# Inverting denominators inside the attentions, four load buffers in the first mixing stage, clipping at the scaled maximum

## The chip, the cores and the metric

The kernel runs on one core of one Trainium2 chip. The measure is the time of one execution on the device in microseconds. A core has TensorE (PE), VectorE (DVE), ScalarE (ACT), GpSimd (POOL), SyncE (SP), which issues most DMAs, and 16 DMA engines.

## The reference

The input x is 8 x 1024 tokens of 256 numbers, float32. Four blocks follow one another, each as `x = x + layernorm(block(layernorm(x)))`:

```python
# 1 attention over a latent of 64, 16 heads of 16, causal softmax
attn = softmax(where(causal, Q @ K.T / 4, -inf)); out = (attn @ V) @ W_o
# 2 feed-forward with ternary weights and a low-rank addition
h = bitlinear(x, w_fc) + gate * (x @ v.T @ fast_b.T @ u.T); out = bitlinear(max(h, 0)**2, w_proj)
# 3 linear attention, second-order features of q and k, causal sums
y = num / (phi_q . cumsum(phi_k) + 1e-5); out = y @ Wo.T
# 4 ternary weights, input scaled by the largest absolute value of the whole tensor
gamma = max(abs(xn)); xq = clip(xn * 128 / gamma, -128 + 1e-5, 128 - 1e-5)
out = (xq @ w_q) * (gamma * beta / 128)
```

Both attentions need a division: the numerator of each head and token by a denominator of that head and token. Block 4 needs one number, gamma, from the whole tensor before its first product.

## The kernel before

`build` (L63) runs passes one after another; between two passes all engines meet, and semaphores of a pass are cleaned up. x stays in SBUF (64 tiles of 128 tokens). The passes are: weights, latent projections, attention with softmax (`attend_pass`, tiles a_*), first mixing stage (`mix_pass`, tiles m_*), feed-forward, features, attention without softmax (tiles b_*), second mixing stage, ternary stage.

**The attentions.** A unit is four heads of one batch, 32 units in all; units run in rounds of three, the last two stand outside of the loop (`all_units`). A unit has 10 steps. TensorE computes the scores of a step two steps ahead of the one that it weighs with the values. In the softmax attention ScalarE takes the exponential and VectorE takes maxima for later units. In the second, ScalarE squares three of four heads and VectorE the fourth (L976, L979); GpSimd masks the steps on the diagonal (L919). Each half of a unit ends with a copy of its sums from PSUM (L938), which SyncE stores in DRAM (L867). These sums hold, for each head, 16 rows of numerators and one of denominators. At its end SyncE waits until the last store has landed.

**The mixing stages.** Work goes in 16 groups of 512 tokens, two for a batch. SyncE loads the denominators of all batches (L1159, 64 KB each), VectorE adds 1e-5 in the second stage (L1210) and inverts (L1212), SyncE stores the inverses in DRAM (L1163) and loads them again, repeated for the 16 rows of each head (L1175). Numerators come through L1170. A group needs two DMAs of numerators and two of inverses, 256 KB each, into one of two buffers. GpSimd multiplies (L1271), TensorE projects (L1324) into one of two sets of banks, VectorE takes statistics from PSUM (L156, L160), ScalarE the root (L166), VectorE the reciprocal (L171), a product of mean and divisor (L1229), the addition to x (L1231) and the shift (L1236). GpSimd's multiplication waits for the loads, for the projection two groups before and for the shift three groups before. The helper `streamed` writes the order: VectorE's step n is add(n-1), then measure(n). The second mixing stage also normalises x for block 4, writes it turned into `flipped` (L1302) and takes the maximum of each group (L1253).

**The ternary stage.** VectorE reduces the 16 maxima to one a partition (L1809), GpSimd reduces over the partitions (L1854), VectorE derives a factor and gains (L1811 to L1815). Per group ScalarE multiplies `flipped` by the factor (L1864), VectorE clips (L1824), TensorE projects (L1891), VectorE takes statistics, root on ScalarE, scales on VectorE (L171, L1836 to L1840), ScalarE copies with scale and offset (L1875), VectorE adds to x (L1847), and SyncE stores the output (L1796). VectorE's step n is clip(n), measure(n-1), add(n-3), scales(n-1). Two sets of PSUM banks alternate: a projection waits for the copy of two groups before.

## Time and profile before

| | us |
|---|---|
| median of 3 runs (2794.3 to 2799.74) | 2794.38 |
| profiled execution, its time / its span | 2794.65 / 2792.9 |
| PE busy in the span | 2454.0 (88%) |
| DVE busy | 2199.0 (79%) |
| ACT busy | 1767.6 (63%) |
| POOL busy | 562.1 (20%) |
| last attention copy to first feed-forward statistics (first mixing stage) | 1154.24 to 1257.74 |
| last copy of the second attention to the ternary stage's first instruction | 2543.59 to 2694.40 |
| ternary stage to the end | 2694.40 to 2792.9 |

Rows of the order of instructions give start, duration (both us), engine, line, operation, output, inputs, shapes and count; in brackets stand the idle time of the engine before it and what ended it. SPq and ACTq are instructions that issue a DMA; their duration is that of the issue.

### The profile page before, as it was taken

Reading aid. Unit: us, or ns where it says so; the run is one execution under the profiler, and the core shown is the slowest. Engines: PE = TensorE matmul, PEld = TensorE weight load, DVE = VectorE, ACT = ScalarE, POOL = GpSimd, SP = SyncE. Lnnn points to the kernel's source line nnn. Section 1 sums busy time; section 2 is a strip of 40 time slices with the busy share of each in tenths; the row PEclk is TensorE's granted clock in tenths of the full one; section 3 lists DMA queues with packets and bytes.
Section 4 is the critical chain, followed back from the end, with each engine's and each line's share of the span. In section 5 each row is a group of like instructions: output and inputs, shape, how many; then the busy total and the mean of one; then the engine's idle time right before and its main releaser. Section 6 shows DMA issues by size and latency. Waiting matters only on the chain. (4 is left out here: it accounts for less than half of the span.)

```text
span 2792.9 us, 57214 instructions
## 1 busy us (share of the span) xinstructions
PE 2454.0 (88%) x15239; PEld 1155.9 (41%) x15239; DVE 2199.0 (79%) x5740; ACT 1767.6 (63%) x2700; POOL 562.1 (20%) x644
## 2 busy tenths in 40 slices
PE   5888999999999999578999997994999999996756
PEld 2442333333333333254666664663333333333645
DVE  6887999899999898286777767996666676666968
ACT  2452666666666666316777755884778788873546
POOL 1543111111111111240000000223222222222300
PEclk8996999999999999898999998997999999998879
DMA  6985353535454543360000002556866776664503
GB/s 187 287 280 122 77 108 81 105 84 103 86 102 87 102 87 83 85 182 1 0 0 0 0 0 68 188 188 184 162 144 142 148 145 144 141 138 118 149 8 117
DMA packets 224106, 309.46 MB, mean 111 GB/s; under 512 B 32416, under 2 KB 170352, under 8 KB 211952
## 3 DMA queue, kind: packets, MB, share of 16 engines
q1 hardware_dynamic: 223616, 307.47, 45.6%
q10 hardware_dynamic: 432, 1.31, 0.2%
q8 instruction: 25, 0.41, 0.1%
q14 instruction: 33, 0.27, 0.0%
HBM read 181.29 MB, written 126.88 MB: 110 GB/s over the span
## 5 line engine op out<-in xcount | busy, mean ns | idle before, releaser
L947 ACT ACTIVATE a_p<-psum 128x1024 f32<-128x1024 f32 (+1 forms) x640 | 567.3, 942 | 303.9 <-PE psum L1045 303.7
L947 ACT ACTIVATE b_p<-psum 128x512 f32<-128x512 f32 (+2 forms) x640 | 444.2, 750 | 145.1 <-PE psum L1045 142.0
L999 DVE CUSTOM_DVE_ANT_0 a_dump<-psum,a_bias 128x128 bf16<-128x128 f32 (+3 forms) x1024 | 446.3, 488 | 56.5 <-PE psum L1034 48.1
L997 DVE TENSOR_REDUCE a_peak<-psum 128x1 f32<-128x512 f32 x512 | 334.7, 688 | 27.6 <-PE psum L1034 25.0
L976 DVE COPY b_twin<-psum 128x512 f32<-128x512 f32 (+1 forms) x320 | 204.0, 637 | 164.5 <-PE psum L1045 161.2
L1045 PE MATMUL psum<-b_qs,b_ks 96*128 96x512 bf16 (+3 forms) x1536 | 307.1, 330 | 28.6 <-DMA b_vs<-values 28.6
L1061 PE MATMUL psum<-b_p,b_vs 128*32 128x512 f32 (+3 forms) x3072 | 314.7, 497 | 6.3 <-POOL b_p L919 6.2
L919 POOL TENSOR_SCALAR_AFFINE_SELECT a_p<-a_p 128x512 f32<-128x512 f32 x256 | 162.3, 634 | 753.7 <-ACT a_p L947 742.0
L1034 PE MATMUL psum<-a_ks,a_qs 96*128 96x128 bf16 (+2 forms) x1008 | 277.4, 333 | 19.3 <-DVE a_peak L999 13.9
L919 POOL TENSOR_SCALAR_AFFINE_SELECT b_p<-b_p 128x512 f32<-128x512 f32 x256 | 159.3, 634 | 441.1 <-DVE b_p L979 429.8
L1045 PE MATMUL psum<-a_qs,a_ks 98*128 98x512 bf16 x1008 | 234.2, 328 | 13.0 <-DMA a_qs<-a_rows 10.8
L1045 PEld LDWEIGHTS psum<-b_qs,b_ks 96*128 96x128 bf16 x1536 | 115.3, 98 | 291.0 <-issue 168.8
L979 DVE SCALAR_TENSOR_TENSOR b_p<-psum,b_twin 128x512 f32<-128x512 f32 (+1 forms) x320 | 204.4, 639 | 33.3
L1522 PE MATMUL psum<-f_xt,w_fc 128*128 128x512 f32 x512 | 225.3, 598 | 3.0 <-ACT f_hid L1463 2.8
L1061 PE MATMUL psum<-a_p,a_vs 128*32 128x512 f32 x2016 | 205.8, 496 | 0.5 <-POOL a_p L919 0.3
L1666 POOL TENSOR_TENSOR g_parts<-g_rest,g_parts 128x2048 bf16<-128x2048 f32 x16 | 66.0, 4127 | 629.7 <-DVE g_parts L1654 629.7
L1324 PE MATMUL psum<-wo,m_att 128*128 128x256 f32 x512 | 127.4, 406 | 58.5 <-POOL m_att L1271 40.0
L1034 PEld LDWEIGHTS psum<-a_ks,a_qs 96*128 96x128 bf16 x1008 | 83.9, 97 | 219.6 <-DVE a_peak L999 121.6
L1533 PE MATMUL psum<-w_proj,f_parts 128*128 128x256 bf16 x1536 | 170.3, 273 | 1.4 <-DVE f_scaled L1411 1.4
L1034 PE MATMUL psum<-first_k,first_q 96*128 96x128 bf16 (+3 forms) x528 | 151.4, 345 | 18.6 <-SPq L878 8.3
L1533 PEld LDWEIGHTS psum<-w_proj,f_parts 128*128 128x128 bf16 x1536 | 150.2, 98 | 19.4 <-DVE f_scaled L1411 1.7
L1400 DVE TENSOR_TENSOR f_rest<-f_sq,f_parts 128x512 f32<-128x512 f32 x128 | 88.5, 691 | 77.0 <-ACT f_sq L1471 76.0
(197 smaller groups left out, 3647.3 us busy)
## 6 DMA issues: line engine op xcount, KB each, us to landing
qk_parts<-l_parts SPq DMA_DIRECT2D x96, 256.0 KB, 3.2
qk_parts<-g_parts SPq DMA_DIRECT2D x96, 256.0 KB, 2.6
values<-l_vx SPq DMA_DIRECT2D x64, 256.0 KB, 3.4
sums<-a_osb SPq DMA_DIRECT2D x64, 256.0 KB, 2.1
m_num<-sums SPq DMA_DIRECT2D x64, 256.0 KB, 3.8
m_inv<-reciprocals SPq DMA_DIRECT2D x64, 256.0 KB, 4.6
values<-g_vx SPq DMA_DIRECT2D x64, 256.0 KB, 3.0
sums<-b_osb SPq DMA_DIRECT2D x64, 256.0 KB, 2.1
```

The costliest lines, as they stand in the source:

```text
L919: pool.affine_select(out=diag, in_=diag, compare_op=ALU.is_ge, fill=0.0, base=0, pattern=[[0, HPU], [1, P]], channel_multiplier=-1).then_i ...
L947: act.activation(p[s % SLOTS][:, 2 * k:2 * k + heads, cols], m.psum[:, at:at + heads, cols], ACT.Exp if softmax else ACT.Square, scale=z.D ...
L976: dve.tensor_copy(twin[s % 2][:, cols], bank).then_inc(twin_ready, 1)
L979: dve.scalar_tensor_tensor(out=p[s % SLOTS][:, 3, cols], in0=bank, scalar=1.0 / z.DK, in1=twin[s % 2][:, cols], op0=ALU.mult, op1=ALU.mult ...
L997: last = dve.tensor_reduce(dst, piece, AX.X, ALU.max)
L999: last = dve.tensor_tensor_reduce(dump[c % SRING][:, at:at + w], piece, bias[:, 512 - w:], 1.0, NEG, ALU.add, ALU.max, dst)
L1034: last = pe.matmul(m.bank[SB + c % SRING][:, at:at + w], qs[r][0:STACK, hd, qt * P:(qt + 1) * P], ks[r][0:STACK, hd, h * 512:h * 512 + w], ...
L1045: last = pe.matmul(m.bank[score_bank(r, s, hd)][:, at:at + w], ks[r][OPERAND, hd, kt * P:(kt + 1) * P], qs[r][OPERAND, hd, h * 512 + q:h * ...
L1061: last = pe.matmul(m.bank[OB[h]][32 * hd:32 * hd + 32, q:q + w], vs[r][:, kt, 32 * hd:32 * hd + 32], p[s % SLOTS][:, hd, at:at + w], start ...
L1324: last = pe.matmul(bank, att[u][:, c, t * P:(t + 1) * P], wo[:, c, :], start=(c == 0), stop=(c == DC - 1))
L1522: last = pe.matmul(m.bank[F0 + j % 4], m.w_fc[:, c, j * P:(j + 1) * P], xt[u][:, c, :], start=(c == 0), stop=(c == DC - 1))
L1533: last = pe.matmul(bank, parts[u][:, part, j, t * P:(t + 1) * P], m.w_proj[:, j, :], start=(part == j == 0), stop=(part == PARTS - 1 and j ...
```

## The change

The diff does four things.

1. The stores' semaphores, the buffers of the copied sums (`osb`) and a tile for seven batches' denominators become resident. An attention no longer waits for its last store; the mixing stage does.
2. Within each attention SyncE loads the denominators of batches 0 to 6 before unit 30 (`load_sums`) and stores their inverses in unit 31, between its two stores of sums (`store_inverses`). VectorE inverts after its last maxima in the softmax attention; in the other one after steps 5, 7 and 9 of unit 30 and 1, 3, 5 and 7 of unit 31. The mixing stage does only batch 7 itself. ScalarE issues the first two groups' inverse loads, SyncE all others.
3. In the first mixing stage the numerators and the inverses have four buffers instead of two. In the second there are still two.
4. In the ternary stage the enlargement is left out: `flipped` is clipped directly at plus and minus gamma x (128 - 1e-5) / 128. Over the partitions the maximum is found by a matmul of ones with the identity times the maxima, and a reduction from PSUM.

```diff
@@ attend_pass, SyncE
+                if not ahead:
+                    store_inverses()
                 store(n, 1)
+            def load_sums():
+                for h in range(2):
+                    sp.wait_ge(stored[h], STORED * (z.UPB * z.EARLY + 1))
+                for b in range(z.EARLY):
+                    sp.dma_start(m.dens[:, b, :], denominators(z, m, b)).then_inc(sums_loaded, 16)
+            def store_inverses():
+                for b in range(z.EARLY):
+                    sp.wait_ge(inverted, b + 1)
+                    sp.dma_start(inverses(z, m, b), m.dens[:, b, :]).then_inc(inverses_stored, 16)
-            all_units(sp, unit)
-            for h in range(2):
-                sp.wait_ge(stored[h], STORED * (UNITS + 1))
+            all_units(sp, unit, load_sums)
@@ attend_pass, VectorE
+        def invert(dve, b):
+            dve.wait_ge(sums_loaded, 16 * z.EARLY)
+            if not softmax:
+                dve.tensor_scalar(m.dens[:, b, :], m.dens[:, b, :], EPS, None, ALU.add).then_inc(padded, 1)
+                dve.wait_ge(padded, b + 1)
+            dve.reciprocal(m.dens[:, b, :], m.dens[:, b, :]).then_inc(inverted, 1)
+                        if not far and ahead and s % 2 and s // 2 >= 2:
+                            invert(dve, s // 2 - 2)
+                        if not ahead and s % 2 and s // 2 + 3 < z.EARLY:
+                            invert(dve, s // 2 + 3)
@@ softmax, after the last unit's maxima
+            for b in range(z.EARLY):
+                invert(dve, b)
@@ mix_pass
+        DEPTH = 4 if flipped is None else 2
+            def load(i, u, e, by_scalar=False):
+                k = buffer_of(u, e)
+                if DEPTH == 2 or not (isinstance(i, int) and i < 2):
+                    sp.wait_ge(att_ready, 2 * i + u + 3 - DEPTH)
...
+            for h in range(2):
+                sp.wait_ge(sums_stored[h], 16 * z.UNITS)
+            for u in range(2):
+                load(0, u, 0, by_scalar=True)
+            for h in range(2):
+                sp.wait_ge(sums_stored[h], 16 * (z.UNITS + 1))
+            sp.dma_start(final, denominators(z, m, z.EARLY)).then_inc(last_loaded, 16)
+            sp.wait_ge(inverses_stored, 16 * z.EARLY)
+            batch(1, 1)
+            sp.wait_ge(inverted, 1)
+            sp.dma_start(inverses(z, m, z.EARLY), final).then_inc(last_stored, 16)
...
@@ mix_pass, ScalarE
+            act.wait_ge(inverses_stored, 16 * z.EARLY)
+            for u in range(2):
+                load_inv(act, 0, u, buffer_of(u, 0))
@@ ternary_pass
+            did(dve.tensor_reduce(peak[:, :], m.peaks[:, :], AX.X, ALU.max))
+            dve.tensor_scalar(spread[:, :], m.ident[:, :], peak[:, 0:1], None, ALU.mult).then_inc(spread_ready, 1)
+            dve.tensor_tensor(w_mean2[:, :], m.w_mean[:, :], m.w_mean[:, :], ALU.mult).then_inc(w_mean2_ready, 1)
+            dve.wait_ge(peaks_ready, 1)
+            did(dve.tensor_reduce(gamma[:, :], all_peaks, AX.X, ALU.max))
+            dve.tensor_scalar(most[:, :], gamma[:, :], (QB - EPS) / QB, None, ALU.mult).then_inc(setup, 1)
+            dve.tensor_scalar(least[:, :], gamma[:, :], (EPS - QB) / QB, None, ALU.mult).then_inc(setup, 1)
             def clip(i, u):
                 n = 2 * i + u
-                dve.wait_ge(enlarged, n + 1)
                 dve.wait_ge(y_ready, n + 1)
-                dve.tensor_scalar(xt[u][:, :, :], large[u][:, :, :], EPS - QB, QB - EPS, ALU.max, ALU.min
-                                  ).then_inc(xt_ready, 1)
+                dve.tensor_scalar(xt[u][:, :, :], flipped[:, bass.ds(n, 1), :, :].rearrange("p n c t -> p (n c) t"),
+                                  least[:, 0:1], most[:, 0:1], ALU.max, ALU.min).then_inc(xt_ready, 1)
-            pool.wait_ge(peak_ready, 1)
-            pool.partition_all_reduce(gamma[:, :], peak[:, :], P, bass.bass_isa.ReduceOp.max).then_inc(gamma_ready, 1)
+            pool.memset(ones[:, :], 1.0).then_inc(ones_ready, 1)
-            streamed(act, GROUPS, (0, enlarge), (2, sums), (1, root))
+            streamed(act, GROUPS, (2, sums), (1, root))
+            pe.matmul(all_peaks, ones[:, :], spread[:, :], start=True, stop=True).then_inc(peaks_ready, 1)
```

## Rows read from the trace of the kernel before

**Rows 1.** Busy time by engine (us, instructions), clock, DMA share, one stretch
```profile
1187.00:1252.00 65.00, 51.58 (x223) 40.92 (x221) 57.11 (x208) 13.15 (x21) 30.08 (x13) 1.00 0.71 196
```

**Rows 2.** Order of instructions, end of first attention, start of first mixing stage
```profile
1154.24 0.60 ACT L938 ACTIVATE a_osb<-psum 128x512 f32<-128x512 f32 x1 [2.10 <-PE psum L1061]
...
1157.96 0.66 SPq L1159 DMA_DIRECT2D m_dens<-sums  x1
...
1160.63 0.95 DVE L1212 RECIPROCAL m_dens<-m_dens 128x128 f32<-128x128 f32 x1 [37.51 <-DMA m_dens<-sums]
...
1166.97 2.80 SPq L1175 DMA_DIRECT2D m_inv<-reciprocals  x4
...
1171.95 4.64 POOL L1271 TENSOR_TENSOR m_att<-m_num,m_inv 128x1024 f32<-128x1024 f32 x2 [18.83 <-DMA m_inv<-reciprocals]
...
1180.04 1.42 DVE L156 BATCH_NORM_STATS2 m_raw<-psum 128x6 f32<-128x256 f32 x4 [5.49 <-PE psum L1324]
```

**Rows 3.** The same view, middle and end of the first mixing stage
```profile
1186.58 2.35 POOL L1271 TENSOR_TENSOR m_att<-m_num,m_inv 128x1024 f32<-128x1024 f32 x1 [1.74 <-DVE shift L1236]
...
1192.39 2.35 POOL L1271 TENSOR_TENSOR m_att<-m_num,m_inv 128x1024 f32<-128x1024 f32 x1 [3.46 <-DMA m_inv<-reciprocals]
...
1193.27 1.48 DVE L1229 TENSOR_TENSOR m_moved<-m_mv,m_rs 128x4 f32<-128x4 f32 x1
...
1247.91 1.42 DVE L156 BATCH_NORM_STATS2 m_raw<-psum 128x6 f32<-128x256 f32 x4
...
1252.21 1.42 DVE L156 BATCH_NORM_STATS2 m_raw<-psum 128x6 f32<-128x256 f32 x4
```

**Rows 4.** Busy time of line L1229 alone (VectorE), first and second mixing stage
```profile
1155.00:1256.00 101.00, 10.42 (x16) 0.90 0.65 180
2544.00:2694.00 150.00, 4.08 (x16) 0.82 0.42 121
```

**Rows 5.** Tile a_osb: its stores (ns min/median/max), first and last start
```profile
L867 SPq DMA_DIRECT2D sums<-a_osb x64: 332/358/387, 272.6 to 1154.9; - x64
...
DMA to landing us min/median/max: 2.0/2.1/8.1
```

**Rows 6.** DMA queues from 1187 to 1250 us: packets, MB, share of 16 engines
```profile
q1 hardware_dynamic: 7430, 12.73, 73.0%
```

**Rows 7.** Tile m_dens: its inversions and additions (ns min/median/max)
```profile
L1212 DVE RECIPROCAL m_dens<-m_dens x16: 894/953/954, 1160.6 to 2566.7; 128x128 f32<-128x128 f32 x16
...
L1210 DVE TENSOR_SCALAR m_dens<-m_dens x8: 162/196/1635, 2549.5 to 2566.5; 128x128 f32<-128x128 f32 x8
```

**Rows 8.** Order of instructions, end of second attention, start of second mixing stage
```profile
2547.20 0.63 SPq L1159 DMA_DIRECT2D m_dens<-sums  x1
...
2560.90 4.64 POOL L1271 TENSOR_TENSOR m_att<-m_num,m_inv 128x1024 f32<-128x1024 f32 x2 [18.43 <-DMA m_inv<-reciprocals]
...
2569.09 1.42 DVE L156 BATCH_NORM_STATS2 m_raw<-psum 128x6 f32<-128x256 f32 x4 [1.41 <-PE psum L1324]
```

**Rows 9.** Order of instructions, start of the ternary stage
```profile
2694.40 0.17 DVE L1809 TENSOR_REDUCE t_peak<-peaks 128x1 f32<-128x16 f32 x1 [0.89 <-PEq L72]
...
2699.95 0.38 POOL L1854 PARTITION_ALL_REDUCE t_gamma<-t_peak  x1 [35.85 <-issue]
...
2703.54 9.06 PE L1891 MATMUL psum<-w_ter,t_xt 128*128 128x256 f32 x32 [12.76 <-DVE t_xt L1824]
```

**Rows 10.** Groups of instructions: busy us, mean ns, idle before
```profile
L373 DVE TENSOR_SCALAR proj_w<-proj,half 128x1024 f32<-128x1024 f32 x2 | 1.5, 752 | 0.0
...
L1253 DVE TENSOR_REDUCE peaks<-flipped (+1 forms) x16 | 19.5, 1218 | 4.6 <-ACT flipped L1302 3.3
```

**Rows 11.** Order of instructions, late in the ternary stage
```profile
2766.22 1.93 ACT L1875 ACTIVATE t_zt<-psum,t_offset,t_grs 128x256 f32<-128x256 f32 x4 [0.64 <-DVE t_offset L1840]
...
2776.01 1.93 ACT L1875 ACTIVATE t_zt<-psum,t_offset,t_grs 128x256 f32<-128x256 f32 x4 [0.65 <-DVE t_offset L1840]
```

**Rows 12.** Groups of instructions again, the second attention's copies
```profile
L976 DVE COPY b_twin<-psum 128x512 f32<-128x512 f32 (+1 forms) x320 | 204.0, 637 | 164.5 <-PE psum L1045 161.2
```

More of the change, by code:

```diff
@@ L120, in __init__ @@
         self.shift = sb("shift", [P, z.TILES])
+        self.dens = sb("dens", [P, z.EARLY, P])
+        self.osb = [sb(f"osb{u}", [P, 512]) for u in range(2)]
         self.psum = ctx.enter_context(nc.psum_tensor("psum", [P, 8, 512], F32))
@@ L1172, in load_inv @@
[L1172 to L1181 removed]
+                    sp.dma_start(num[k][:, c, :], src.rearrange("h d t -> d h t")).then_inc(loaded[k], 16)
@@ L1182, in batch @@
+                if not by_scalar:
+                    load_inv(sp, i, u, k)
+            def batch(i, e):
                 for u in range(2):
-                    load_num(2 * k + e, u)
-                    load_inv(2 * k + e, u)
-            load_dens(0)
+                    load(i, u, e)
+            for h in range(2):
+                sp.wait_ge(sums_stored[h], 16 * z.UNITS)
             for u in range(2):
-                load_num(0, u)
-            store(0, 0)
-            for b in range(1, z.B):
-                load_dens(b)
@@ L1192, in _ @@
-            sp.wait_ge(inv_stored[0], 16)
-            for u in range(2):
-                load_inv(0, u)
-            store(1, 1)
-            batch(0, 1, True)
+                load(0, u, 0, by_scalar=True)
[5 more added lines that the diff above has]
+            sp.wait_ge(inverted, 1)
```

134 lines of the change are left out of this document (64 added, 70 removed).

## The prediction

> **What bounds the kernel now.** I read first the table of stages, because the change touches three short stages of a long span, then the order of instructions at the start and in the middle of each. In the first mixing stage no engine is full: in its middle 65 us VectorE is busy 57.11, TensorE 51.58 and the DMA engines 0.71 of the time [rows 1]. The shares hide two different costs. The stage starts late: the last copy of sums ends at 1154.84, VectorE's first statistics of a group begin at 1180.04 [rows 2]. In between stands a chain of transfers and one inversion: sums stored and awaited, denominators loaded, inverted, stored, loaded back broadcast, multiplied on GpSimd. The 15 intervals between the first statistics and the sixteenth at 1252.21 are then (1252.21 - 1180.04) / 15 = 4.81 us long, while the last, with all transfers done, is 1252.21 - 1247.91 = 4.30 [rows 2, 3]. The difference is a collision. A multiplication that waited for the DMA of inverses starts at 1192.39 and runs 2.35 us; the tiny product of mean and divisor beside it takes 1.48 us, though the 16 products of the second mixing stage average 4.08 / 16 = 0.26 [rows 3, 4]. Where the multiplication is released by the shift instead, as at 1186.58, it lies under the statistics, as all but one do in the second mixing stage, and the product is free. All 16 products took 10.42 us in the first stage [rows 4]; at 0.16 each they would take 2.6, so 7.8 us are lost there, which is the 15 x (4.81 - 4.30) = 7.7 of the intervals.
>
> **First mixing stage, start.** SyncE no longer waits for the last store before the stage ends. That store lands 2.1 us after its issue at 1154.9 [rows 5], so 1157.0; the next stage's first DMA is at 1157.96: about 1.0 us of stage change. Now SyncE is free once the store is issued, 0.36 us after 1154.9 [rows 5], and its first load goes at 1156.2. The numerators go from SyncE, the inverses of batches 0 to 6 (stored during the attention) from ScalarE, at the same time. Before, the second of the inverse loads was issued at 1166.97 + 0.70 = 1167.67 and the multiplication began at 1171.95, 4.28 later [rows 2]. The new second load goes at 1156.9, but 1 MB is now needed instead of 0.5. What the DMA engines carry at full share: of the 63 us from 1187 on, 12.73 MB at a share of 0.73 [rows 6], so 12.73 / (63 x 0.73) = 277 GB/s, and the additional 0.52 MB take 1.9 us at most. I take 1.4 of it: 1156.9 + 4.28 + 1.4 = 1162.6, against 1171.95: **9.3 us less**. From the multiplication to the statistics (8.1 us) nothing changes. Bounds: 7 us, if the requests of the second group, issued right behind, take half of the bandwidth, and 10.7, if the extra half costs nothing.
>
> The last batch's denominators are loaded, inverted and stored within the stage; the 64 KB are wanted only by groups 14 and 15, 60 us later: nothing. Of inverting batches 0 to 6 inside the first attention I also count nothing: VectorE stands idle for 37.51 us before its first instruction of the mixing stage [rows 2], which is more than 7 x 0.95 = 6.7 [rows 7]; SyncE's seven loads go while it would wait for the second last unit's results, its seven stores some 9 us ahead of the last one. Uncovered, the inversions would cost those 6.7.
>
> **First mixing stage, middle.** Four load buffers let a load start three groups ahead. A group needs four transfers, 1.05 MB, 3.8 us at 277 GB/s; the interval is 4.30. So the loads lie ready, each multiplication is released by the shift, and the collision goes. What is late next is VectorE itself, busy nearly throughout the 4.30. I take 4.33 for 15 intervals: 15 x (4.81 - 4.33) = **7.2 us less**. Bounds: 0, if the transfers hold the pace, and 7.7.
>
> **Second mixing stage.** Only its start changes, the buffers stay two. First DMA at 2547.20, first multiplication at 2560.90, first statistics at 2569.09 [rows 8]. The first loads can go 1157.96 - 1156.2 = 1.7 us sooner as in the first stage, at 2545.5, and by the same sum the multiplication starts at 2545.5 + 0.7 + 4.28 + 1.4 = 2551.9: **9.0 us less**. VectorE's own inversions, which before went on to the first statistics, are no cover any more and no wait either. The product loses only 4.08 - 2.6 = 1.5 us in the whole stage [rows 4], in the third multiplication, whose load still follows the first one: it stays. Bounds 6.5 and 10.3.
>
> **Ternary stage.** Before: maximum at 2694.40, GpSimd's reduction over partitions not before 2699.95, five small operations, enlargement on ScalarE, clipping, first product at 2703.54 [rows 9]. After: maximum; identity times maximum, 0.3 us, a little above the 0.20 of a 128x128 addition [rows 7]; a matmul, under 0.5 (32 slow ones take 9.06, so 0.28 each, plus its weights); a reduction from PSUM, some 0.3; two scalings, 0.2 each; clipping, 0.75 as a 128x1024 comparison with a scalar per partition [rows 9, 10]. With about 0.07 us for each of six waits this is 0.2 + 0.3 + 0.5 + 0.3 + 0.4 + 0.75 + 0.4 = 2.9, so the product starts at 2697.3: **6.2 us less**. Bounds 5 and 6.8.
> In its middle the enlargement leaves ScalarE, but it isn't on the loop. From one copy to SBUF to the next of the same banks, two groups later, are 2776.01 - 2766.22 = 9.79 us [rows 11]: copy, products, statistics, addition, scales, without the clip, which is done while the products run: 0. If two scalars per partition cost the clip its double rate, it takes 1.22 like the reduction over 1024 elements instead of 0.75 [rows 10]; even without any cover that is 16 x 0.47 = 7.5 us more. I take 0, as the nearest row keeps the rate.
>
> **Second attention.** The one part that costs. VectorE gets seven inversions in the last two units, every second step: an addition, 0.20, and a reciprocal, 0.95 [rows 7], 1.15 in all. It is idle 164.5 / 320 = 0.51 us per step [rows 12], so 1.03 of each 1.15 is refilled over two steps, but each one first makes the next copy 0.65 late, and the masks and products of the unit's edges follow VectorE directly. The sums needed are loaded only after the unit before, just in time. Bounds: 0.5, and 7 x 1.15 = 8.1 if nothing absorbs; I take **2.0 us more**, since TensorE runs two steps ahead of what it weighs.
> The addition has been seen to take 1.64 us beside a GpSimd operation [rows 7]. The Trainium skill (SBUF — State Buffer, "Who interferes with whom") says that such a tensor-scalar operation and GpSimd take one port pair by turns, for a whole instruction, so each addition could stand behind a mask. By the page alone the edges would pay more than my 2.0, by the typical row nothing.
>
> **Sum.** -9.3 - 7.2 - 9.0 - 6.2 + 2.0 = -29.7 us. The profiled execution took 2794.65 (span 2792.9), 0.3 above the median of 2794.38: I predict 2794.4 - 29.7 = **2764.7 us**.
>
> **Rivals.**
> A, transfers hold the first mixing stage: deep buffers, but the DMA engines give no more than the mean of 12.73 / 63 = 202 GB/s [rows 6], 1.05 MB take 5.2 us, and the interval stays 4.81. For it: bursts already near full share. Against: the share of 0.73 leaves room. Time 2764.7 + 7.2 = 2771.9.
> B, the starts gain less, because two groups are asked for at once from two queues and both land together, 2 x 1.05 MB at 277 GB/s instead of one: 7 and 6.5 instead of 9.3 and 9.0: 2769.5; with a part of A 2773.
> C, the second attention pays all: +6.1, 2770.8. For it the edges without idle time, against it the 0.51 per step.
> D, the other side: the collision of multiplication and product becomes the rule in the first mixing stage. If each multiplication, with loads always ready, started where it meets the product, every interval would be 4.30 + 2.1 = 6.4, 15 x (6.4 - 4.81) = 24 us more where I count 7.2 less: 2764.7 + 31 = 2796. It decides once the mean stall exceeds (29.7 + 0.3) / 15 = 2.0 us. Against it: the code waits for the shift, and products of 0.26 us where that wait ends last, in the second mixing stage [rows 4].
> E, the change doesn't do what it says in the second mixing stage: the last inverses, stored near the end of the attention, land after the stage has begun (3 to 4 us more): 2768.
>
> **Chances.** Forecast 0.6 (its own range 2760 to 2769), A 0.1, B 0.12, C 0.08, E 0.06, D 0.02, and 0.02 that more is gained. Range 2758 to 2774. A difference of 0.2%, 5.6 us, can be told from none: all but D lie beyond it. With something for what I don't see: faster 0.96, same 0.02, slower 0.02.
>
> **What would show it.** First statistics of the mixing stages about 9 us sooner after the last copy of sums; 16 products of mean and divisor together under 3 us in the first; intervals of 4.3; 2.9 us from maximum to first ternary product; ternary intervals unchanged at 4.9; the last two units of the second attention 2 us longer. Multiplications that still wait for DMA would speak for A, a product of 2 us in each group for D.

## The result, and the profile after

The changed kernel takes 2771.2 us (median of four runs, 2768.88 to 2772.11), beside 2794.34 us for the kernel before on the same chip (2788.91 to 2799.74): 0.9916 of it, 95% interval 0.9896 to 0.9936. Forecast were 2764.7 us and a range of 2758 to 2774. The profiled execution took 2772.11, its span is 2770.4 (before 2794.65 and 2792.9).

The table gives the same marks in both traces. "Last copy" is the start of the last copy of sums on ScalarE.

| stretch (us) | before | after | difference | forecast |
|---|---|---|---|---|
| up to the last copy of the first attention | 1154.24 | 1154.00 | -0.24 | 0 |
| last copy to first statistics, first mixing stage | 25.80 | 18.54 | -7.26 | -9.3 |
| 15 intervals of the first mixing stage | 72.17 | 64.59 | -7.58 | -7.2 |
| to the second attention's first copy of scores | 706.47 | 705.78 | -0.69 | 0 |
| to the last copy of the second attention | 584.91 | 589.65 | +4.74 | +2.0 |
| last copy to first statistics, second mixing stage | 25.50 | 18.19 | -7.31 | -9.0 |
| to the maximum | 125.31 | 123.60 | -1.71 | 0 |
| maximum to the last addition, ternary stage | 94.38 | 91.85 | -2.53 | -6.2 |
| sum of the differences | | | -22.6 | -29.7 |

The first mixing stage's start, in order of time, answers to [rows 2] (start, duration, engine, line, operation; idle time and its end in brackets):

```profile
1154.00 0.60 ACT L977 ACTIVATE osb<-psum 128x512 f32<-128x512 f32 x1 [2.10 <-PE psum L1106]
...
1155.94 2.85 ACTq L1209 DMA_DIRECT2D m_inv<-reciprocals  x4
...
1155.99 3.17 SPq L1222 DMA_DIRECT2D m_num<-sums  x4
...
1164.07 2.34 POOL L1309 TENSOR_TENSOR m_att<-m_num,m_inv 128x1024 f32<-128x1024 f32 x1 [11.18 <-DMA m_num<-sums]
...
1166.55 9.41 PE L1371 MATMUL psum<-wo,m_att 128*128 128x256 f32 x32 [12.60 <-POOL m_att L1309]
...
1172.54 1.43 DVE L172 BATCH_NORM_STATS2 m_raw<-psum 128x6 f32<-128x256 f32 x4 [3.45 <-PE psum L1371]
```

The first loads go 1.9 us after the last copy, where the first DMA before went 3.7 after it, and the inversions are gone from the chain. But the multiplication starts 8.1 us after the first load's issue, not the 6.4 that I worked out. The pace of the stage is what was expected: from the fourth on, every multiplication is released by the shift. Line L1267 is the tiny product of mean and divisor; the columns are the stretch, its length, VectorE's busy time, granted clock of TensorE (1.00 is 2.4 GHz, 0.50 is 1.2), DMA share, GB/s, for the first and the second mixing stage, as in [rows 4]:

```profile
1154.00:1240.00 86.00, 2.60 (x16) 0.92 0.82 200
2532.00:2675.00 143.00, 2.60 (x16) 0.85 0.43 120
```

All 32 of these small products now take 0.16 us. The one collision in the second stage, which I had left standing, is gone too: 4.08 - 2.60 = 1.5 us of the 1.71 there. The queue of the loads over 58 us, beside [rows 6], and how long they are under way:

```profile
q1 hardware_dynamic: 6305, 11.46, 81.5%
...
m_num<-sums SPq DMA_DIRECT2D x18, 256.0 KB, 8.9
m_inv<-reciprocals SPq DMA_DIRECT2D x18, 256.0 KB, 9.8
```

In the first 45 us of it the queue moves some 258 GB/s without a gap (I had counted on 277) and is then done; with four buffers a landing of 9 us is no wait.

The second mixing stage's start, beside [rows 8]:

```profile
2532.56 0.60 ACT L977 ACTIVATE osb<-psum 128x512 f32<-128x512 f32 x1 [4.92 <-PE psum L1106]
...
2541.60 2.34 POOL L1309 TENSOR_TENSOR m_att<-m_num,m_inv 128x1024 f32<-128x1024 f32 x1 [11.44 <-DMA m_inv<-reciprocals]
...
2545.63 2.34 POOL L1309 TENSOR_TENSOR m_att<-m_num,m_inv 128x1024 f32<-128x1024 f32 x1 [1.69 <-DMA m_inv<-reciprocals]
...
2545.66 2.39 DVE L1255 TENSOR_SCALAR m_final<-m_final 128x128 f32<-128x128 f32 x1 [16.85 <-DMA m_final<-sums]
...
2550.75 1.42 DVE L172 BATCH_NORM_STATS2 m_raw<-psum 128x6 f32<-128x256 f32 x4 [1.71 <-PE psum L1371]
```

The addition of 2.39 us runs from 2545.66 to 2548.05; the multiplication beside it from 2545.63 to 2547.97. In the attention the same addition takes 0.22. It delays only batch 7's inverses here. The Trainium skill (SBUF — State Buffer, "Who interferes with whom") says that a tensor-scalar operation in a two-port mode and GpSimd exclude one another for a whole instruction, and that the one issued first wins. These two rows agree.

The second attention's end. First the waits of TensorE in its last 38 us (engine, line, what for, us in total, times, longest), then TensorE's order:

```profile
PE psum L1106 <- POOL b_p L958: 2.9, 4, 1.8
PE psum L1090 <- DVE b_p L1018: 0.8, 2, 0.5
```

```profile
2502.33 0.23 DVE L869 TENSOR_SCALAR dens<-dens 128x128 f32<-128x128 f32 x1 [1.22 <-DMA dens<-sums]
...
2529.72 2.79 PE L1106 MATMUL psum<-b_p,b_vs 128*32 128x384 f32 x24 [1.84 <-POOL b_p L958]
```

And the granted clock over two stretches there, before and behind the pause (length, busy time with count of PE, weight loads, DVE, ACT, POOL, then granted clock, DMA share, GB/s):

```profile
2526.00:2528.70 2.70, 1.88 (x16) 0.47 (x12) 2.49 (x5) 1.40 (x4) 0.87 (x2) 1.00 0.08 24
...
2529.70:2532.60 2.90, 2.79 (x24) 1.09 (x24) 0.00 (x0) 0.04 (x1) 0.46 (x1) 0.50 0.03 6
```

The last 24 products run at the lower level (0.50, 1.2 GHz) and take 2.79 us. The kernel before runs the same 24 in 1.50, behind a pause of 0.76 and not 1.84:

```profile
2542.03 1.50 PE L1061 MATMUL psum<-b_p,b_vs 128*32 128x384 f32 x24 [0.76 <-POOL b_p L919]
```

The ternary stage's start answers to [rows 9]:

```profile
2674.35 0.17 DVE L1857 TENSOR_REDUCE t_peak<-peaks 128x1 f32<-128x16 f32 x1 [0.86 <-PEq L73]
...
2674.99 0.77 PE L1926 MATMUL psum<-t_spread,t_ones 128*128 128x128 f32 x2 [4.23 <-DVE t_spread L1858]
...
2676.59 1.53 DVE L1871 TENSOR_SCALAR t_xt<-flipped,t_least,t_most 128x1024 f32<-128x1024 f32 x2 [0.25 <-DVE t_least L1863]
...
2677.54 9.96 PE L1934 MATMUL psum<-w_ter,t_xt 128*128 128x256 f32 x32 [1.78 <-DVE t_xt L1871]
...
2689.76 8.86 PE L1934 MATMUL psum<-w_ter,t_xt 128*128 128x256 f32 x32 [2.27 <-ACT t_zt L1915]
2701.04 3.72 PE L1934 MATMUL psum<-w_ter,t_xt 128*128 128x256 f32 x16 [2.42 <-ACT t_zt L1915]
```

From maximum to first product are 3.19 us (9.14 before). A group is 16 products in these rows, and 16 at the higher level take 3.72, so 32 take 7.4; here the first pair of groups takes 9.96 and the second pair, groups three and four, 8.86. The clock in three stretches, columns as above:

```profile
2675.00:2683.00 8.00, 6.22 (x15) 4.86 (x16) 2.04 (x5) 0.00 (x0) 0.00 (x0) 0.50 0.01 2
2683.00:2689.00 6.00, 4.50 (x21) 3.57 (x19) 3.91 (x15) 1.61 (x4) 0.00 (x0) 0.98 0.00 1
2689.80:2693.00 3.20, 3.20 (x8) 2.60 (x9) 1.84 (x9) 1.66 (x4) 0.00 (x0) 0.54 0.00 0
```

In the kernel before the first products ran at 0.50 for their first 3.9 us only, and then at 1.00:

```profile
2703.50:2707.40 3.90, 3.86 (x9) 3.15 (x10) 0.69 (x1) 0.22 (x1) 0.00 (x0) 0.50 0.01 2
2707.50:2715.00 7.50, 5.58 (x26) 4.61 (x25) 4.76 (x20) 3.30 (x6) 0.00 (x0) 1.00 0.00 0
```

So the questions were: does TensorE's clock take the missing 3.7 us of the ternary stage and part of the 4.7 in the second attention; what do the inversions cost; what holds the mixing stages' first loads.

### The profile page after: what moved, and what is told of

The parts are those of the page before. It is cut to its first block and busy times, and to the rows that moved or that the text cites. A ratio compares the mean times of both kernels' runs of the same rounds, so it can differ in the third digit from the quotient of the medians.

```text
span 2770.4 us, 57128 instructions
## 1 busy us (share of the span) xinstructions
PE 2456.8 (89%) x15241; PEld 1158.9 (42%) x15241; DVE 2189.2 (79%) x5740; ACT 1751.3 (63%) x2684; POOL 562.9 (20%) x644
## 5 line engine op out<-in xcount | busy, mean ns | idle before, releaser
L1090 PE MATMUL psum<-b_qs,b_ks 96*128 96x512 bf16 (+3 forms) x1536 | 307.8, 330 | 29.7 <-DMA b_vs<-values 28.9
```

Source lines behind the costliest of these rows:

```text
L1090: last = pe.matmul(m.bank[score_bank(r, s, hd)][:, at:at + w], ks[r][OPERAND, hd, kt * P:(kt + 1) * P], qs[r][OPERAND, hd, h * 512 + q:h * ...
```

## The experiments

All are edits of the changed kernel but the last two, which edit the kernel before. Stage times are taken at the marks of the table, each from one trace. Stretches that no edit touches differ between traces too: the one up to the last copy of the first attention took 1151.3 to 1154.2 us. The first four ran on one chip, the next four on another, e8 to e10 on a third, e11 on a fourth; the kernel before had 2793.45, 2792.74, 2793.96 and 2793.53 us there.

**e0_again**, the changed kernel itself, unedited.

> The changed kernel, unchanged, once more. The profile of the first time shows two drops of TensorE's granted clock to its lower level that the kernel before does not show in these places: in the last products of the second attention (24 products in 2.79 us instead of 1.50) and in the third and fourth group of the ternary stage (32 products in 8.86 us). If these drops belong to the program, they are here again at the same places; if they depend on where a short pause of TensorE happens to fall, one or both are absent or elsewhere, and the stage concerned is 1.3 us (attention) or about 2 us (ternary) shorter. Time 2769 to 2772 us.

2770.37 us (2768.8 to 2772.25), ratio 0.9918 [0.9901, 0.9934]. The marks repeat: starts +18.18 and +18.44, intervals 64.58, second attention 589.43, ternary stage 91.77, with the 24 products again 2.79 and the second pair of ternary groups 8.86. It is the base for the others.

**e1_no_inversions_b**, VectorE's inversions of batches 0 to 6 in the second attention left out (their denominators are stored as loaded, and SyncE's stores wait for the loads in place of the inversions):

```diff
                 for b in range(z.EARLY):
-                    sp.wait_ge(inverted, b + 1)
+                    if softmax:
+                        sp.wait_ge(inverted, b + 1)
+                    else:
+                        sp.wait_ge(sums_loaded, 16 * z.EARLY)
...
-                        if not far and ahead and s % 2 and s // 2 >= 2:
-                            invert(dve, s // 2 - 2)
-                        if not ahead and s % 2 and s // 2 + 3 < z.EARLY:
-                            invert(dve, s // 2 + 3)
```

> Leaves out VectorE's seven additions and reciprocals in the second attention; the loads of the denominators and the seven stores stay (so the second mixing stage multiplies by denominators). The second attention grew by 4.7 us. Theory 1, VectorE's order: the inversions hold up the copies, masks and products behind them; then 3.4 us go, and with them the pause before the last products, so the clock drop of 1.3 us too: 4.7 us less, 2766.5. Rival, the seven loads and stores themselves disturb SyncE's queue and the transfers: then most of the 4.7 us stay and the time is above 2769.

2767.19 us (2762.6 to 2768.76), 0.9902 [0.9885, 0.9918]. The second attention takes 585.74, that is 3.69 less, and its last products run at the full level behind a short pause:

```profile
2527.63 1.50 PE L1105 MATMUL psum<-b_p,b_vs 128*32 128x384 f32 x24 [0.77 <-POOL b_p L961]
```

Of the 3.69 the clock has 2.79 - 1.50 = 1.29 and the inversions 2.4, near the forecast 2.0.

**e2_two_buffers**, `DEPTH = 2` in both mixing stages.

> Two load buffers in the first mixing stage as well. Theory, the buffers free the multiplication from the transfers: intervals between the statistics go back from 4.31 to about 4.8 us, the product of mean and divisor is again held up (10 us for 16 instead of 2.6), 7.5 us more, 2778.5; the start of the stage stays as it is. Rival, that earlier inverses alone removed the collision (no stores of inverses between the loads any more): intervals stay under 4.5 and the time under 2774.

2773.59 us (2773.15 to 2774.06), 0.993 [0.9913, 0.9946]. The 15 intervals take 68.98 (64.58 with four buffers, 72.17 before). Line L1267 in the first mixing stage, columns as above:

```profile
1154.00:1240.00 86.00, 7.29 (x15) 0.92 0.68 199
```

(The 16th of these products lies behind the window; all 16 take 7.45.) So the collision comes back with two buffers, though less often. The intervals are 4.60 us long, between the theory's 4.8 and the rival's 4.5. The time rose by 3.2 and not by 4.4, in part because the second attention took 587.60 in this trace, 1.8 less than in e0_again, its last products at the higher level. Of the 7.6 us that the middle gained, the four buffers have 4.4; the other 3.2 came with the rest of the change. That this is the stores of inverses no longer queued between the loads is my reading; no run isolates it.

**e3_old_ternary**, the ternary stage of the kernel before in the changed kernel.

> The ternary stage of the kernel before, all else as in the changed one. The stage gained 2.5 us where 6.2 were forecast. If the new stage is worth what its own profile says, the time is 2.5 us above the changed kernel, 2773.7; if the missing 3.7 us are a matter of where TensorE's clock falls, the gain differs from execution to execution and the mean difference is anywhere between 2 and 6 us, with the first product 9.1 us after the maximum instead of 3.2 in either case.

2773.99 us (2771.76 to 2779.03), 0.9933 [0.9917, 0.995]. Its ternary stage takes 94.02, against 91.77: the new one is worth 2.25 us here, as the traces said, and not 6.2. What is missing must be in the stage itself. The time rose by 3.6, more than the stage: in this trace the first multiplication of the first mixing stage starts 10.0 us after its first load, where e0_again, with the same code there, has 7.5.

**e4_sliced_b**, the same inversions in halves, most of them one to a step:

```diff
-                        if not far and ahead and s % 2 and s // 2 >= 2:
-                            invert(dve, s // 2 - 2)
-                        if not ahead and s % 2 and s // 2 + 3 < z.EARLY:
-                            invert(dve, s // 2 + 3)
+                        if not far and ahead:
+                            if s == 6:
+                                pad(dve)
+                            for j in {7: (0,), 8: (1,), 9: (2, 3)}.get(s, ()):
+                                invert_half(dve, j)
+                        if not ahead:
+                            for j in ((s + 4,) if s < 8 else (12, 13) if s == 9 else ()):
+                                invert_half(dve, j)
```

`pad` adds EPS to the denominators of all seven batches, `invert_half` takes the reciprocal of 64 columns; SyncE's stores wait for both halves.

> The second attention's inversions are cut up: EPS is added to all seven groups' sums in one instruction in the last but one unit, and each group's reciprocal is taken in two halves of 64 columns, one half a step, in place of .22 + .95 us every other step. In e1_no_inversions_b the stage fell from 589.5 to 585.7. Theory 1 (an inversion of 1.2 us is longer than the slack that VectorE has before TensorE waits for it, and a half of .5 us fits into it): the stage takes 586 to 587 us, the products at the stage's end run at the higher clock in 1.50 and not 2.79, and the time falls by 2.5 to 3.5 us, to about 2767.5. Theory 2 (VectorE has no slack in these steps, only the sum of its work counts): two reciprocals of half the columns cost as much as one and a fixed cost each, the stage stays at 589 to 590.5, and the time at 2770 to 2771.5. A last inverse stored late would show as a first product of the second mixing stage more than 9.3 us after the last copy of the attention.

2766.66 us (2765.47 to 2767.43), 0.991 [0.9893, 0.9926]; second attention 584.23. VectorE's halves in the last 38 us (busy us, mean ns, idle before; the one addition takes 0.62), then TensorE's waits at the end, and its last products:

```profile
L878 DVE RECIPROCAL dens<-dens 128x64 f32<-128x64 f32 x14 | 7.3, 536 | 0.0
```

```profile
PE psum L1123 <- POOL b_p L971: 1.2, 3, 0.8
```

```profile
2524.80 1.50 PE L1123 MATMUL psum<-b_p,b_vs 128*32 128x384 f32 x24 [0.76 <-POOL b_p L971]
```

VectorE does as much as before (7.3 + 0.6 = 7.9 us for 6.7 + 1.5 = 8.2), and yet TensorE's waits fall from 3.7 to 1.2 us. Theory 1 holds against theory 2: what cost was not the sum of the work but the length of one inversion against the slack of a step (and the spacing that goes with it; the two were not taken apart). That the stage fell by 5.2, below e1, is not all the slicing's: the first 20 us of this stage ran at a mean clock of 0.92 here and 0.84 in e0_again, which is up to 20 x 0.08 = 1.6 us. In e8, with the same inversions and 0.84, the stage took 585.71, as long as without any inversions (585.74 in e1): in halves they cost nothing that can be seen.

**e5_warm_ternary**, products nobody reads ahead of the ternary stage:

```diff
                 streamed(pe, GROUPS, (0, project), (2, turn))
+                for _ in range(5):
+                    pe.matmul(m.bank[0][:, 0:z.D], m.ident[:, :], wo[:, 0, :], start=True, stop=True)
...
             pe.matmul(all_peaks, ones[:, :], spread[:, :], start=True, stop=True).then_inc(peaks_ready, 1)
+            for _ in range(3):
+                pe.matmul(m.bank[5][:, 0:z.D], m.ident[:, :], m.w_ter[:, 0, :], start=True, stop=True)
```

> TensorE gets work whose result nobody reads in the pause before the ternary stage: five products of 128 columns by 512 behind the last projection of the second mixing stage, three more behind the product that spreads the peaks. Clock theory (the ternary start gained 2.5 us less than forecast because TensorE's granted clock is .50 in its first 9.96 us group of products, and again in the third group at 8.86): the first 32 products take about 7.2 us and not 9.96, the fall in the third group is gone or elsewhere, the ternary stage falls from 91.8 to 87.5 to 89 us and the time to 2766 to 2768. Rival (the stage start is held by VectorE's chain from the peak to the first clipped rows and by the transfers, and the clock only fills that time): the first statistics come as late as in e0_again, 9.6 us after the peak, and the time stays within 1 us of 2770.5. A second rival: the work put in delays the spread of the peaks by more than it gives, first clipped rows later than 3.2 us after the peak.

2766.06 us (2765.5 to 2766.8), 0.9908 [0.9891, 0.9924]; ternary stage 87.02 for 91.77.

```profile
2668.36 3.37 PE L1386 MATMUL psum<-wo,ident 128*128 128x256 f32 x10
...
2673.51 1.46 PE L1930 MATMUL psum<-w_ter,ident 128*128 128x256 f32 x6
2675.45 7.17 PE L1938 MATMUL psum<-w_ter,t_xt 128*128 128x256 f32 x32 [0.48 <-DVE t_xt L1873]
2684.89 3.72 PE L1938 MATMUL psum<-w_ter,t_xt 128*128 128x256 f32 x16 [2.26 <-ACT t_zt L1917]
```

(Each product of the edit stands in the rows as two.) The first 32 products take 7.17, the third group alone 3.72, so the second fall is gone, and the first statistics come at +6.63 us for +9.61. The clock theory holds; the first product itself is only 0.3 us sooner.

**e6_warm_mix**, the same at the start of both mixing stages:

```diff
+            for _ in range(20 if flipped is None else 19):
+                pe.matmul(m.bank[T0][:, 0:z.D], m.ident[:, :], wo[:, 0, :], start=True, stop=True)
```

> TensorE gets work whose result nobody reads while each mixing stage waits for its first rows: 20 products in the first, 19 in the second, into a bank that the first projection then overwrites. Clock theory (the first projection's 32 products take 5.9 us in the first and 6.7 us in the second mixing stage from the product of the rows to the statistics because the clock is .50 after the pause): the first statistics come 2 to 3 us sooner after the last copy of the attention, 16 us in place of 18.2 in the first and 15.5 in place of 18.4 in the second, and the time falls by 4 to 5.5 us, to 2765 to 2767. Rival (the second group's rows are the later ones, and what the first projection gives back is waited for by the second): first statistics sooner, but the sixteenth as late as in e0_again, and the time within 1.5 us of 2770.5.

2766.72 us (2766.58 to 2767.31), 0.9909 [0.9892, 0.9925]. The first statistics come at +15.46 and +17.28 (+18.18 and +18.44), and then the 15 intervals take 66.71 for 64.58, the second stage to the maximum 125.21 for 123.64: net -0.6 and +0.4 us. The rival's sign came, the sixteenth statistics hardly sooner, but not for its reason. It is the collision of [rows 3], once in each stage: the third multiplication, now released by a load, starts just ahead of the tiny product of mean and divisor (L1267) or runs when it comes. The first two rows are the first stage's, the others the second's:

```profile
1170.56 2.35 POOL L1309 TENSOR_TENSOR m_att<-m_num,m_inv 128x1024 f32<-128x1024 f32 x1 [1.79 <-DMA m_inv<-reciprocals]
1170.59 2.33 DVE L1267 TENSOR_TENSOR m_moved<-m_mv,m_rs 128x4 f32<-128x4 f32 x1
...
2546.19 2.34 POOL L1309 TENSOR_TENSOR m_att<-m_num,m_inv 128x1024 f32<-128x1024 f32 x1 [2.94 <-DMA m_inv<-reciprocals]
...
2546.69 1.86 DVE L1267 TENSOR_TENSOR m_moved<-m_mv,m_rs 128x4 f32<-128x4 f32 x1
```

At 0.16 us each the two would be 2.17 and 1.70 shorter, and the stages behind the first statistics took 2.13 and 1.57 more. In e9, with the same products at the start, the collision hardly comes, and the gain stays.

The time is nevertheless 3.7 us lower, and 3.2 of that lie in the second attention, 586.24 for 589.43, which this edit does not touch. In its first 20 us the mean granted clock was 0.90 for 0.84 (up to 20 x 0.06 = 1.2 us), and its last products ran at the full level (1.3 us), although the pause ahead of them was as long as in e0_again:

```profile
2525.39 1.50 PE L1106 MATMUL psum<-b_p,b_vs 128*32 128x384 f32 x24 [1.83 <-POOL b_p L958]
```

The same 24 products stand behind the same pause of 1.83 to 1.84 us in seven traces. They took 2.57 to 2.79 in five (after, e0, e3, e5, e7) and 1.50 in two (e2, e6). Behind the pause of 0.76 to 0.77 us that seven other traces have (before, e1, e4, e8 to e11) they took 1.50 each time. So the fall came behind the longer pause alone, but that pause does not decide it. The Trainium skill (TensorE: Matmul & The Clock Gate, "Part 1: The HAM clock gate (the "warmup" mystery)") says that the chip judges activity on a clock of its own, which no kernel restarts, so that the same work can meet the change at another place; these seven traces are in keeping with that and do not prove it.

**e7_hold_second**, the second group's first loads wait for the first group's landing:

```diff
-            for u in range(2):
-                load(0, u, 0, by_scalar=True)
+            load(0, 0, 0, by_scalar=True)
+            sp.wait_ge(loaded[buffer_of(0, 0)], LOADED)
+            load(0, 1, 0, by_scalar=True)
...
-            for u in range(2):
-                load_inv(act, 0, u, buffer_of(u, 0))
+            load_inv(act, 0, 0, buffer_of(0, 0))
+            act.wait_ge(loaded[buffer_of(0, 0)], LOADED)
+            load_inv(act, 0, 1, buffer_of(1, 0))
```

> The loads of the second group of rows in each mixing stage are not issued until the first group's have landed. Bandwidth theory (the first product comes 9.4 us after the attention's last copy, of which 7 to 9 us is a landing, because two groups' transfers, about 2 MB, share the DMA engines and all end together): the first group's rows land in half to two thirds of the time, the first product comes 1.5 to 3 us sooner, at +6.5 to +8 us in both stages, and the statistics of the first group with it; the second group's come no sooner than now, so that the time falls by 0 to 3 us. Rival (the landing is the fixed latency of a load and the number of descriptors a queue carries one after the other): the first product comes within .5 us of +9.4, the second group's rows 2 us or more later than now, and the time rises by 1 to 3 us.

2770.49 us (2768.88 to 2772.45), 0.9923 [0.9907, 0.994]. The first multiplication starts at +9.59 and +8.95 (+9.41 and +9.50). From the first load's issue to it 7.6 and 7.1 us pass (7.5 and 7.6 in e0_again; 7.2 to 8.1 in the ten traces with both groups asked for, but for the 10.0 of e3): my bandwidth theory, which wanted 1.5 to 3 us less, falls. Of the rival two signs came, the same landing and the second group's multiplication 2.5 and 2.9 us later, counted from the first load. The third did not: the time stayed. The first statistics came at +18.36 and +19.83, and the 15 intervals took 65.68, 1.1 more, as long as one collision cost (a product of 1.30 at 1172.15); what offsets this lies in stretches that the edit does not touch. The DMA engines alone with one group's 1.05 MB, from the first load at 1153.2 to the multiplication at 1160.85 (last columns: DMA share, GB/s):

```profile
1154.00:1155.00 1.00, 0.00 (x0) 0.00 (x0) 0.00 (x0) 0.00 (x0) 0.00 (x0) 0.93 0.19 51
1155.00:1156.00 1.00, 0.00 (x0) 0.00 (x0) 0.00 (x0) 0.00 (x0) 0.00 (x0) 0.50 0.99 168
...
1157.00:1158.00 1.00, 0.00 (x0) 0.00 (x0) 0.00 (x0) 0.00 (x0) 0.00 (x0) 0.50 1.04 352
...
1159.50:1160.80 1.30, 0.00 (x0) 0.00 (x0) 0.00 (x0) 0.00 (x0) 0.00 (x0) 0.50 0.06 17
```

Some 1.8 us pass before the engines are full, 4.5 are transfer, and 1.3 pass with nearly nothing moved before GpSimd starts. That idle tail was in no term of mine for two queues. The Trainium skill (DMA: Bandwidth & Descriptors, "Anatomy of one DMA — SWDGE (gpsimd) path") puts most of a DMA's fixed cost behind its last byte. On these queues, which are others than that section's, the tail is 1.3 us, and the beginning of 1.8 is longer.

**e8_two_mended**, e4 and e5 together.

> The changed kernel with both mends that moved a stage: the inversions of the second attention in halves (e4_sliced_b) and products into unread banks ahead of the ternary stage (e5_warm_ternary). If the two act on separate stages they add: second attention 584 us (589.4 in e0_again), ternary stage 87 us (91.8), everything else as in e0_again, so 2770.4 - 5.2 - 4.8 = 2760.4 us, between 2759 and 2763. Rival (part of what e4 and e5 gained came from where the falls of TensorE's granted clock happen to lie, and does not add): 2764 to 2766, with a fall of the clock in the second attention's end or in the third group of the ternary stage.

2764.5 us (2763.15 to 2765.53), 0.9897 [0.9881, 0.9914]. Second attention 585.71, last products 1.50, ternary stage 87.09; its profiled execution is 2764.19, span 2762.4. Against e0_again's span of 2769.7 the two stages give -3.7 - 4.7 = -8.4, the second mixing stage +1.0. The rival's time came, and in part for its reason: the 1.6 us or so that e4 owed to the clock at the stage's start are missing. Neither fall that it named as a sign came.

**e9_three_mended**, e8 and e6 together.

> As e8_two_mended, and with the 20 and 19 unread products at the start of the mixing stages (e6_warm_mix). In e6 the first statistics came 2.7 and 1.2 us sooner and the stage behind them took 2.1 and 1.6 us longer, and the second attention took 586.2 in place of 589.4 with no fall of the clock at its end. Theory (the mixing stages' starts are held by the second group's rows, and e6 gained only by that stretch of the second attention, which the halved inversions already have): no faster than e8 by more than 1 us, so 2759.5 to 2763. Rival (the warm start is worth what the first statistics gain): 2756 to 2758.

2763.75 us (2760.47 to 2764.54), 0.9895 [0.9879, 0.9912]: by the times not told apart from e8. The profiled execution is the fastest of the four, 2760.47, span 2758.8, and in it the warm starts are worth something. The stretch from the last copy to the sixteenth statistics takes 80.94 for e8's 83.07, the one from the last copy to the maximum in the second stage 141.41 for 143.10, 2.1 and 1.7 us less. The tiny product that took 2.33 and 1.86 in e6 takes 0.40 and 0.16 here:

```profile
1170.93 0.40 DVE L1284 TENSOR_TENSOR m_moved<-m_mv,m_rs 128x4 f32<-128x4 f32 x1
```

So the theory on record, that the starts are held by the second group's rows, does not fit this trace, though its forecast, at most 1 us faster than e8, came for the median. Whether the other three executions, 3.2 to 4.1 us slower, had the collision isn't known. The third pair of ternary groups, five and six, pays for a fall of the clock here, which e8 has nowhere in the stage:

```profile
2687.77 8.86 PE L1957 MATMUL psum<-w_ter,t_xt 128*128 128x256 f32 x32 [1.91 <-ACT t_zt L1936]
```

**e10_before_warm**, the kernel before with 20 products behind its second mixing stage's last projection.

> The kernel before with 20 products into an unread bank behind the last projection of the second mixing stage, so that TensorE works through the pause of 12.76 us ahead of its ternary stage. Clock theory (both kernels pay for the pause, the kernel before 3.9 us of its first products at the lower clock, the changed one twice as much): its ternary stage falls from 94.4 to 91.5 to 93 us, so that with the clock up on both sides the changed ternary stage (87.0 in e5_warm_ternary) is 4.5 to 6 us shorter, near the 6.2 forecast, and the time is 2791 to 2792.5. Rival (the products of the first group end behind another chain in the kernel before): the stage stays at 94 to 94.5 and the time at 2793.5.

2799.42 us (2796.14 to 2803.38, ten runs), 1.0018 [1.0008, 1.0028]: slower, and the test failed. Between two passes all engines meet, so the maximum waited for the products:

```profile
2703.29 0.17 DVE L1811 TENSOR_REDUCE t_peak<-peaks 128x1 f32<-128x16 f32 x1 [8.43 <-PEq L72]
...
2712.54 8.78 PE L1893 MATMUL psum<-w_ter,t_xt 128*128 128x256 f32 x32 [10.12 <-DVE t_xt L1826]
```

And in the 10.12 us behind them the clock had fallen again (0.50 from 2705.7 to 2715.7), so that the stage took 94.20.

**e11_before_warm_late**, the kernel before with 15 such products at the start of the ternary stage itself:

```diff
             pe.sem_inc(y_ready, 2)
+            for _ in range(15):
+                pe.matmul(m.bank[5][:, 0:z.D], m.ident[:, :], m.w_ter[:, 0, :], start=True, stop=True)
```

> The kernel before with 15 products into an unread bank at the start of its ternary stage's TensorE program, where e10_before_warm had 20 ahead of the stage's start (they held the peak's reduction for 8 us and the clock fell again in the 10.12 us behind them). At .67 us each for the first 3.9 us and .46 to .49 from there they fill 8.2 of the 9.1 us between the peak and the first product. Theory (the two ternary starts differ by the spread of the peak and the enlarged rows, about as forecast, and the clock took the difference away in the changed kernel): the first 32 products take 7.2 us and not 9.06, the ternary stage 92.3 to 92.8 us, against 87.0 in e5_warm_ternary, so that with the clock up on both sides the change is worth 5.3 to 5.8 us there, near the 6.2 forecast; the time is 2791.5 to 2793. Rival (the start of before does not wait for its products): the stage stays at 94.2 to 94.5, and of the change's forecast more than the clock is missing or less.

2790.87 us (2789.08 to 2796.74, ten runs), 0.9995 [0.9985, 1.0004]; ternary stage 92.44, for 94.38 in before.

```profile
2691.59 8.36 PE L1885 MATMUL psum<-w_ter,ident 128*128 128x256 f32 x30 [3.77 <-PEq L72]
2700.55 7.17 PE L1893 MATMUL psum<-w_ter,t_xt 128*128 128x256 f32 x32 [0.60 <-DVE t_xt L1824]
```

With the clock up on both sides the first statistics come 12.85 us after the maximum in the old stage and 6.63 in the new one (e5): 6.22 us, and the whole stage is 92.44 - 87.02 = 5.42 shorter.

## Why the prediction was right, and where it was not

The time lies inside the range, 6.5 us above the forecast and above the forecast's own range by 2. Every term had the right sign, but of five only the middle of the first mixing stage had the right size, and the range held in part by luck: four terms were off to the same side, by 10.1 us together, and what I had put at nothing gave 3.0 back. By its steps:

- **First mixing stage, middle** (-7.2): right, -7.58, and by the mechanism named: multiplications released by the shift, products of 0.16 us, intervals of 4.31. But the four buffers have only 4.4 of it (e2). Rivals A and D are refuted: the loads run at 258 GB/s without a gap (277 was my figure for full share) and behind the second group the stage waits for none, and no product is held. D's collision is still there when a load releases a multiplication (e2, e6, e7), though in none of these in each group.
- **The two starts** (-9.3 and -9.0): -7.26 and -7.31, 2.0 and 1.7 short, the size of rival B. The loads left at the moment forecast (1.94 us after the last copy; 1.96 forecast). The step that failed is "4.28 + 1.4" for the landing of 1 MB: with the 0.7 ahead of it I had 6.4 us from the first load to the multiplication, and 8.1 and 7.2 passed, 1.7 and 0.8 more. Rival B's reason, two groups that share the DMA engines, is not the cause (e7: 7.6 and 7.1 with one group alone); what fills the time is a slow beginning, 4.5 us of transfer and the tail of 1.3. The other 0.4 and 1.0 are TensorE's: from multiplication to statistics are 8.47 and 9.15 us, for 8.09 and 8.19 before, the first 32 products taking 9.41 and 10.17 for 9.03 and 9.21, more of them at the lower level. A warm start gives that back (e6), and the stage keeps it where the third multiplication does not meet the tiny product (2.1 and 1.7 us in e9).
- **Second mixing stage, collision**: forecast to stay, gone, -1.5. The third multiplication, from 2550.98 to 2553.33, is at its end when the tiny product comes at 2553.28; in e1 and e4, with the same code there, that product takes 0.40 and 0.51.
- **Second attention** (+2.0): the term was mis-sized, +4.74. The inversions by themselves cost 2.4 (e1), near the forecast, and in pieces half as long, one a step, nothing (e4, e8). Another 1.3 is TensorE's clock, which falls behind the pause that comes with the last inversions (0.77 without them, 1.84 with them); up to 20 x (0.88 - 0.84) = 0.8 more is the clock in the stage's first 20 us. I had no term for a clock that falls, and took TensorE's pace as given. Rival C, all 8.1, did not come. The additions took 0.22 or 0.23 throughout, but this says little on the conflict with GpSimd's masks: six of the seven ran while no mask did, and the seventh met the last 0.05 us of one.
- **Ternary stage** (-6.2): the chain from maximum to first product was right to 0.3 us (3.19 for 2.9), the gain was not: -2.53. The step that failed is the unspoken one that a first product 6 us sooner brings everything behind it 6 us sooner. The first statistics came 5.05 us sooner after the maximum (9.73 for 14.78), as the first 32 products took 9.96 in place of 9.06: 1.2 short. The 15 intervals behind them took 75.09 for 72.57, 2.5 more. Of these 1.7 go with the second fall (73.36 in e5, where there is none) and 0.8 remain, e5 against the 72.56 of e11. e5 and e11 give 6.22 us at the first statistics once both run at the higher level. "I take 0" for the clip may be what misses the 0.8: it takes 812 ns, for 694 before, but no run isolates it.
- **Rival E** did not come: SyncE's seven stores of inverses were issued by 2527, before the attention's end, and the first loads went at once.

By terms, the starts lacked 2.0 + 1.7, the ternary stage 3.7, the attention 2.7, in all 10.1; the collision (1.5), the middle (0.4) and the stretches elsewhere (1.1) gave 3.0 back. That is the 7.1 between -29.7 and the -22.6 at the marks of the two traces; the medians differ by 23.1.

## What to carry to other kernels

When an edit shortens a wait ahead of a stage, ask at which clock TensorE will start there: a shorter chain can still leave the pause that lowers it, and a few products nobody reads, put where no other engine waits for them, took 4.7 us from the ternary stage here (e5). Work moved onto a nearly full engine should be cut to pieces no longer than that engine's slack per step (0.51 us here): the same 8 us of inversions cost 2.4 us in pieces of 1.15 and close to nothing in pieces of 0.54. A gain at a stage's start can be lost to a collision that only the new timing brings (2.2 us in e6), so the first few groups are to be read as well as the first. And a load's time ahead of its first use is to be read as beginning, transfer and tail: here 1.8, 4.5 and 1.3 us, and with half the bytes asked for (e7) the first use came 0.5 us sooner at most.

## What was not expected of the hardware

- The granted clock fell behind a pause of TensorE of only 1.84 us in five of seven traces and not in two, with the same instructions on both sides. What decides it is open.
- In the ternary stage the clock fell again 12 us after the first products, among groups of 3.72 us with pauses of 2.3 us, in the second pair of groups (after, e0, e1, e6) or in the third (e2, e4, e7, e9), and not at all in e5 and e8. The old stage had no such fall (before, e3, e10, e11).
- 7.2 to 8.1 us from the first load to the multiplication where 2 MB were asked for, and once 10.0 with the same code (e3); 7.6 and 7.1 where the first 1 MB went alone.
- A product of 128x4 numbers, 0.16 us by itself, took 2.33 when GpSimd's multiplication had started 0.03 us ahead of it (e6).
